# Spreading the second feed-forward blocks of a hybrid layer over its chunk steps, pass by pass

## What is computed

```python
x = x + rwkv(layernorm(x))      # projections, a recurrence along time, projection
x = x + ffn(layernorm(x))       # "F1": 512 -> 1376 gate and up, silu(gate)*up, 1376 -> 512
x = x + mamba(layernorm(x))     # projections, conv of 4 taps, state scan with 16 states, gate, projection
x = x + ffn(layernorm(x))       # "F2": the same weights as F1
```

## Time and profile before

| | |
|---|---|
| median of 3 runs | 3535.84 us (3535.15 to 3536.14) |
| the profiled execution, its own time | 3535.06 us |
| its span, first to last instruction | 3533.3 us |
| granted TensorE clock, mean | 0.969 |

### The profile page before, as it was taken

The page is one execution under the profiler, slowest core; times in us unless marked ns, Lnnn a source line. Parts: engine busy times, 40 slices in busy tenths (PEclk is TensorE's granted clock), DMA queues, the critical chain, the costliest instruction groups (busy, mean ns, idle before and its releaser), DMA issues.

```text
span 3533.3 us, 46726 instructions
## 1 busy us (share of the span) xinstructions
PE 3233.1 (92%) x12672; PEld 2341.7 (66%) x12672; DVE 3141.1 (89%) x5676; ACT 2602.2 (74%) x5260; POOL 2473.7 (70%) x1959
## 2 busy tenths in 40 slices
PE   4889899899999999999999999999999999976738
PEld 4666676676767676767767676767676767754425
DVE  5899995499999999999999999999999999999990
ACT  4777774487878787878787878788787878766650
POOL 0343444296969696969696969696969696968680
PEclk9999999999999999999999999999999999988879
DMA  3122213111111111111111112121112010111110
GB/s 107 60 75 85 77 63 129 54 34 39 42 39 41 40 40 40 42 37 42 39 41 40 42 37 48 33 49 31 52 27 58 24 55 25 54 25 36 26 35 6
DMA packets 119380, 165.39 MB, mean 47 GB/s; under 512 B 8544, under 2 KB 84192, under 8 KB 118624
## 3 DMA queue, kind: packets, MB, share of 16 engines
q1 hardware_dynamic: 119136, 162.63, 16.5%
HBM read 128.39 MB, written 25.69 MB: 44 GB/s over the span
## 4 chain that ended last, share of the span: by engine, by line
POOL 46%; issue 21%; DVE 21%; PE 6%; ACT 4%; DMA 1%; DVEq 1%; POOLq 0%; SPq 0%; ACTq 0%
POOL dBu L907 24%; POOL yacc L920 17%; DVE D L1412 6%; DVE U L1361 4%; PE W L1162 3%; DVE prod L1431 1%; DVE dBu L1392 1%; PE W L1196 1%; DVE U L1404 1%; DVE D L1434 1%; DVE sgm L1345 1%; DVE delta L1399 1%; POOL NV L305 1%; POOL EO L293 1%; POOL MX L278 1%
## 5 line engine op out<-in xcount | busy, mean ns | idle before, releaser
L907 POOL TENSOR_TENSOR dBu<-U,BC 128x512 f32<-128x512 f32 x1024 | 1297.8, 1279 | 359.9 <-DMA BC<-bc_scratch 247.3
L1412 DVE TENSOR_TENSOR_SCAN D<-D,hc,dBu 128x256 f32<-128x256 f32 x2048 | 1433.5, 738 | 17.5 <-ACT D L1077 17.5
L1162 PE MATMUL W<-nT,wffn 128*128 128x256 f32 x5632 | 1230.9, 381 | 7.8 <-ACT nT L948 7.8
L1162 PEld LDWEIGHTS W<-nT,wffn 128*128 128x128 f32 x5632 | 1063.9, 189 | 181.2 <-issue 18.3
L1077 ACT ACTIVATE D<-delta,A 128x256 f32<-128x256 f32 x2048 | 890.7, 468 | 363.4 <-DVE yacc L1444 338.7
L920 POOL TENSOR_TENSOR yacc<-yacc,prod 128x512 f32<-128x512 f32 x752 | 956.9, 1273 | 175.1 <-DVE prod L1431 171.0
L1196 PE MATMUL W<-wffn,hT 128*128 128x512 f32 (+1 forms) x1408 | 617.6, 595 | 7.9 <-DVE hT L1330 7.9
L1431 DVE TENSOR_TENSOR prod<-D,BC 128x512 f32<-128x512 f32 x752 | 503.8, 670 | 0.0
L1196 PEld LDWEIGHTS W<-wffn,hT 128*128 128x128 f32 (+1 forms) x1408 | 263.1, 190 | 326.2 <-issue 307.6
L1162 PE MATMUL W<-nT,win 128*128 128x256 f32 x2048 | 451.0, 381 | 30.1 <-ACT xext L996 22.8
L1162 PEld LDWEIGHTS W<-nT,win 128*128 128x128 f32 x2048 | 391.3, 191 | 91.1 <-ACT xext L996 23.6
(11 more groups left out here) (128 smaller groups left out, 3036.7 us busy)
## 6 DMA issues: line engine op xcount, KB each, us to landing
BC<-bc_scratch SPq DMA_DIRECT2D x256, 256.0 KB, 4.6
XM<-x_scratch SPq DMA_DIRECT2D x29, 512.0 KB, 6.0
X<-x_scratch SPq DMA_DIRECT2D x17, 512.0 KB, 3.6
ix<-idx SPq DMA_DIRECT2D x33, 255.0 KB, 2.9
X<-x SPq DMA_DIRECT2D x16, 512.0 KB, 3.4
XR<-x SPq DMA_DIRECT2D x16, 512.0 KB, 3.4
x_scratch<-XR SPq DMA_DIRECT2D x16, 512.0 KB, 3.6
out<-X SPq DMA_DIRECT2D x16, 512.0 KB, 2.8
```

The costliest lines, as they stand in the source:

```text
L907: nc.gpsimd.tensor_tensor(dBu[e % 4][:], U[:, 2 * j:2 * j + 2, :], BC[slot][:, 0:1, :].to_broadcast([P, 2, CH]), ALU.mult).then_inc(s_dBu, 1)
L1162: last = T_.matmul(dst, lhsT, rhs, start=(n == 0), stop=(n == len(terms) - 1))
L1412: V.tensor_tensor_scan(D[:, m, :], D[:, m, :], dBu[e % 4][:, m % 2, :], hc[:, n, m:m + 1], ALU.mult, ALU.add).then_inc(s_scan, 1)
```

## The change

The late F2 blocks of steps 2 to 13 are cut between passes. Over six steps five blocks are done: the late part has 6, 4, 3, 2, 1 and 0 passes, and the **rest** of the block (the missing passes and its `down`) stands first in the next step, ahead of the early block. So steps 2 to 13 hold 11/6 blocks on average in place of 2, F2 of chunks 11 to 14 are left over, and steps 14 and 15 hold two blocks each in place of one. The transposed rows of a cut block are kept in a new buffer `nT2`; `dtl`, `bcS` and `dump` share memory to make room, which adds waits on earlier uses. The rows x3 between Mamba and F2 now go through DRAM (`x3_d`): stored behind BC slot 4, loaded again into `X3` for the rest's residual (behind slot 5) and for the late norm. The early rows in `XM` give way to the next Mamba rows, whose norm is now made in the middle of the step (in place, in `XM`), and are loaded a second time for their residual (`early_slot`). The silu, norm and residual places come out of a formula in units of a place.

```diff
-F1_SILU = (10, 13, 16, 19, 22, 24)
-F1_RES = 31
-F2_SILU = (36, 39, 42, 45, 48, 50)
-F2_RES = 56
-L_SUM = 12
-M_SUM = 50
+PASS, HALF, DOWN = 3.15, 1.6, 8.8
+LEAD, LEAD_REST = 6.85, 6.5
...
+        LEAN = NC - 2
+        PART = (NP, 4, 3, 2, 1, 0)
...
         def early(i):
-            return ("F1", 1) if isinstance(i, int) and i == 0 else ("F1", i + 2)
+
+            if i == 0:
+                return "F1", 1
+            return ("F1", i + 2) if i < LEAN else ("F2", 2 * i - NC - 1)
...
+            if i == 1 or i >= LEAN:
+                return ("F2", 0 if i == 1 else 2 * i - NC), NP, True
+            turn_, n = divmod(i - 2, len(PART))
+            return (("F2", (len(PART) - 1) * turn_ + n + 1), PART[n], False) if PART[n] else (None, 0, False)
...
+        def slot(e):
+
+            return -(-e // 4) + 2
...
+                for p in range(first, last):
+                    t += HALF if p == NP - 1 else PASS
+                    out.append(t)
+                return out, t
+
+            t = LEAD
+            at["e_norm"], at["e_evac"] = 0, 6
+            if R_:
+                e, last = ends(LEAD_REST, r, NP)
+                at["r_silu"] = tuple(round(x) for x in e)
+                t = last + DOWN
+                at["r_res"] = round(t - 2.5)
...
+            e, last = ends(t, 0, NP)
+            at["e_silu"] = tuple(round(x) for x in e)
+            at["e_res"] = round(last + DOWN - 2.5)
+            at["xm_slot"] = max(3, slot(at["e_norm"] - 3))
+            at["m_sum"] = 4 * (at["xm_slot"] - 2) + 6
+            at["m_norm"] = at["m_sum"] + 6
+            at["m_evac"] = round(last) + 4
+            at["l_sum"] = max(at["m_norm"] + 2, 18, (at["r_res"] or 0) + 11)
...
+            at["early_slot"] = slot(round(last))
...
+                        if n == 4:
+                            keep_x3(i)
+                        if n == 5:
+                            if R_:
+                                load_x3(i, R_[1])
+                            elif L_:
+                                load_x3(i, L_[1])
+                        if R_ and n == at["r_slot"]:
+                            keep_out(R_, X3)
+                            if L_:
+                                sp.wait_ge(out_stored, 16 * (outs.index(R_) + 1))
+                                load_x3(i, L_[1])
+                        if n == at["early_slot"]:
...
+                            load_early(i)
...
+                    if R_:
+
+                        project(i - 1, 1, 1 - a)
+                        for p in range(n_rest, NP):
...
+                            gate_up(R_, p, nT2)
...
+                        down(R_, [(1, 4, turn_early)])
```

More of the change, by code:

```diff
@@ new lines, in hybrid_block_kernel @@
+        norms, downs = [("F1", 0), ("M", 0)], [("F1", 0)]
+        passes = [(("F1", 0), p) for p in range(NP)]
+        xm_loads, x3_loads = [("x1", 0), ("x1", 2)], [("x1", 1), ("x2", 0)]
+        for i in range(NC):
+            (R_, r_), E_, (L_, l_, whole) = rest(i), early(i), late(i)
+            if R_:
+                passes += [(R_, p) for p in range(r_, NP)]
+                downs.append(R_)
+                x3_loads.append(("rest", R_[1]))
+            norms.append(E_)
+            passes += [(E_, p) for p in range(NP)]
+            downs.append(E_)
+            if i == 0:
+                norms += [L_, ("M", 1)]
+            else:
+                norms += [("M", i + 1)] * (i + 1 < NC) + [L_] * (L_ is not None)
+            passes += [(L_, p) for p in range(l_)]
+            if whole:
+                downs.append(L_)
+            if i:
+                x3_loads += ([("late", L_[1])] if L_ else []) + [("x2", i)]
+                xm_loads += [("x2", i + 1)] * (i + 1 < NC) + [("early", i)]
+            if i + 1 < NC:
+                xm_loads.append(("next", i + 1))
@@ new lines, in hybrid_block_kernel, with gate_side @@
+        LAST_ = ("F2", NC - 1)
+        norms.append(LAST_)
+        passes += [(LAST_, p) for p in range(NP)]
+        downs.append(LAST_)
+        outs = [block for block in downs if block[0] == "F2"]
+        norm_no, down_no = norms.index, downs.index
+        pass_no = lambda block, p: passes.index((block, p))
+        xm_no = lambda what, n: xm_loads.index((what, n))
+        x3_no = lambda what, n: x3_loads.index((what, n))
+        def gate_side(i):
+            (_, r), (_, n, whole) = rest(i), late(i)
+            if whole:
+                return 0
+            if rest(i)[0]:
+                return (NP - r + n) % 2
+            return 1 - n % 2
@@ L833, in step @@
                 def step(i, back, f1, more):
+                    at = places(i)
+                    (R_, _), (L_, _, whole) = rest(i), late(i)
                     if not back:
+                        sp.wait_ge(n_done, TT * (norm_no(("M", 0)) + 1))
                         load_x1(2)
-                    elif more and not f1:
-                        sp.wait_ge(n_done, TT * (norm_no("M", i) + 1))
-                        load_x2(i + 1, NC)
                     sp.wait_ge(m_bcS, i + 1)
@@ L891, in step @@
                 def step(i, back, f1, more):
-                    at = places(f1)
-                    if f1 and not back:
-                        root(norm_no(*early(i)))
+                    at = places(i)
+                    if not back:
+                        root(norm_no(early(i)))
                     def outer(e):
@@ L1053, in step @@
                         soft(j)
[L1054 to L1058, removed]
+                    at = places(i)
+                    E_, (L_, n_late, whole), (R_, n_rest) = early(i), late(i), rest(i)
+                    early_rows, late_rows, mamba_rows = (XM, X3, XM) if back else (X3, XM, X3)
                     def save(e):
@@ new lines, in step @@
+                        if more and e == at["m_norm"]:
+                            if not back:
+                                act.wait_ge(f_h, pass_no(L_, NP - 1) + 1)
+                            slope(norm_no(("M", i + 1)))
+                            norm(norm_no(("M", i + 1)), mamba_rows, XM if back else nrm)
+                        if more and e == at["next_sum"]:
+                            act.wait_ge(xm_loaded, 16 * (xm_no("next", i + 1) + 1))
+                            sums(i, norm_no(early(i + 1)), XM)
@@ L1111, in step @@
+                        if more and e == at["next_sum"] + 1:
+                            squares(norm_no(early(i + 1)), XM)
                         if e == G_LATE:
@@ new lines, in gate_up, with down @@
+                def gate_up(block, p, src):
+                    Wp = W[sides[block, p]]
+                    for half, wt in ((0, wg), (2, wu)):
+                        for m, r in rows(p):
+                            last = chain(Wp[0:r, half + m % 2, :], [(wt[:, k, m * P:m * P + r], src[:, k, :]) for k in range(KH)])
+                    last.then_inc(f_gu, 1)
+                def down(block, turns=()):
+                    done = pass_no(block, NP - 1)
+                    o = W[down_sides[block]][:].rearrange("p (t a) n -> p t (a n)", t=TT)
+                    pe.wait_ge(f_h, done)
+                    for t in range(TT):
+                        for k in range(MI):
+                            for at_t, at_k, what in turns:
+                                if (t, k) == (at_t, at_k):
+                                    pe.wait_ge(f_h, done + 1)
+                                    what()
+                            if t == 0 and k == MI - 1:
+                                pe.wait_ge(f_h, done + 1)
+                            r = LAST if k == MI - 1 else P
+                            last = T_.matmul(o[:, t, :], hT[0:r, k, t * P:(t + 1) * P], wd[0:r, k, :], start=(k == 0), stop=(k == MI - 1))
@@ new lines, in step @@
+                    for p in range(n_late):
+                        if p == 0:
+                            pe.wait_ge(n_T, norm_no(L_) + 1)
+                        elif p == 1:
+                            pe.wait_ge(f_res, down_no(E_) + 1)
+                        else:
+                            pe.wait_ge(f_h, pass_no(L_, p) - 1)
+                        gate_up(L_, p, nT2 if back else nT)
+                    if whole:
+                        down(L_, [] if back else [(1, 6, lambda: turn(norm_no(("M", 1)), f))])
@@ L1369, in step @@
                 def step(i, back, f1, more):
-                    at = places(f1)
+                    at = places(i)
+                    E_, (L_, n_late, whole), (R_, n_rest) = early(i), late(i), rest(i)
+                    early_rows, late_rows = (XM, X3) if back else (X3, XM)
                     for h in range(2):
```

537 lines of the change are left out of this document (313 added, 224 removed).

## The result

The changed kernel takes 3620.94 us (median of 4, 3614.63 to 3621.76) against 3535.52 us: the ratio is 1.0238, 95% interval 1.022 to 1.0255. It is slower, as I had thought likeliest, but by 85 us where I had 12; the range ended at 3562.

A forecast was written before the change was run, and what follows sets the result against it. PE was taken to set the pace, with DVE 5 us behind; small gains and losses per step and -1 for a head summed to +11.7 us, giving a median of 3547.5 us (+0.33%), range 3515 to 3562.

The forecast's parts named there:

- The sum of 11.7 us: Whole kernel: the step changes and a shorter head behind step 14 add up to +11.7 us, median 3547.5.
- my own case: Whole kernel: the main forecast of 3547.5 us, +0.33%, own range 3541 to 3556, chance 0.40.
- PE sets the pace: Step 5's loop: PE busy 144.95 of 145.50 us sets the pace, with DVE only 5 us behind.
- The first bound: Loops of steps 2 to 13: each gains at most its waits, 5.3 us, and what DVE no longer does.
- The waits forecast where squares stand ahead of a silu: Steps 5, 6, 11, 12: squares share a silu's place, ahead of it; the same meeting before cost DVE 2.67 us.
- Where the places put the waits: Steps 1 to 15: DVE waits on PE at residuals; PE's saving shows only after a step's last such meeting.
- this meeting: Steps 1, 2, 8: DVE meets the early down's end at residual place 30, at 72.7 us, hiding M's norm work.
- Steps 14 and 15: Last two loops: one more block gives DVE busy 144.6 and 144.4, waits taken as 4.9: +3.8 and +4.4 us.
- Steps 4 to 7 and 10 to 13: Loops with less PE work: -2.1 in 4 and 10, +0.7 in 5 and 11, +0.6 in 6 and 12, -1.5 in 7 and 13.
- The first (faster, 3515): Rows land in 3.6 us, ACT works off extras in its lead; 3515, or 3500 if residual meetings cost nothing; chance 0.28.
- The second (work only changes its step): DVE, not PE, sets the pace: 8.8 us leave and 8.8 come, so no change, 3536; chance 0.22.
- The third (SP held): SP's queue: a store's or norm's wait delays a BC slot, POOL and DVE wait, 2.8 us in ten steps: 3575; chance 0.10.

The follow-up runs named there:

- Experiment 11: The kernel before, blocks not cut, with early residual, late means, squares and norm, and Mamba means moved to other places: 3512.41 us.
- Experiment 10: The changed kernel with ACT's norm work on one column (not the layer's output) and the fifth silu one place earlier: 3558.63 us.
- experiment 9: The changed kernel with 16 unneeded matmul instructions on TensorE ahead of the early block's last pass, in steps 1 to 15: 3601.05 us.

## Why the prediction was wrong

**Right, or nearly.** The sum of 11.7 us adds up; the upper end of my own case does not (the bounds given make 3558, not 3556). "PE sets the pace" was nearly right: I read it from 144.95 of 145.50 us busy, though DVE never waited for TensorE in that loop. Experiment 11 shows that TensorE's bound is 143.9; the last 1.6 us were DVE's waits for ACT, which TensorE filled with work for the next step. DVE's work does not change (3141.1 us in both). The first bound, that a loop can gain its waits and DVE's saved work, held: the best loop is 140.3 of 145.5. The waits forecast where squares stand ahead of a silu are in the trace at their places, 1.9 us at place 32 of step 5 and 2.8 at 35 of step 6 (I had the 2.67 of the kernel before). So is the wait for x3 at place 13 (5.9; I had 6.2), the waits at the rest's residual (1.9 to 3.3; I had 2.5 in step 4), and DVE's new wait for `XM` behind a DMA in step 5 (1.9; I had 2.5). That the kernel got slower is thus no luck, but these waits are the smaller part of it: 46 of the 86 us lie in steps 1, 2, 8, 14 and 15, where I had 9.

**The step that failed** is the one under "Where the places put the waits": I took TensorE's timeline as free-running up to each residual (72.7 in step 1, 101.5 in step 4) and let DVE's waits on the way be hidden by it ("they cost no more than this meeting hides"). But `down` starts only with the fifth product, which is DVE's and is behind ACT's. In step 1 the products' waits held TensorE for 5.24 us, the lower clock cost 2.8 more, and the meeting came at 80.2. Experiment 10, which takes away ACT's norm work inside the passes and moves the fifth product forward, gives the 72.5 of my sum; experiment 9 shows the clock's part by itself.

**Five terms that were mis-sized or missing.** (1) I gave the fifth silus' shift from 22 to 23 and from 48 to 49 no price at all, though both rows of places stand in the table; it cost 26 us over the kernel. (2) The clock: I had used it only to take 1 us off behind step 14 (that head fell by 0.5); over the fifteen early `down`s it took TensorE 29 us more than at the full clock, and experiment 9, which avoids nearly all of that, was 20 us faster. (3) Steps 14 and 15: I took the waits of a step like 5; they were those of step 1 on top of DVE's larger work, +13.3 and +10.6 for +3.8 and +4.4. (4) Steps 4 to 7 and 10 to 13, where TensorE's saving was to show after the last meeting, met the same chain: TensorE waited 2.6 to 3.6 us ahead of their early `down`, and the loops were 0.3 to 6.0 us longer. (5) The collision that I priced in steps 5 and 6, squares ahead of a silu in one place, also stands at place 19 of steps 1, 2, 8, 14 and 15; I had not seen it there, and it cost DVE 2.28 us at place 18.

**The rivals.** The first (faster, 3515) had the right limit but not for this kernel: its case without waits at the residuals gave 3500, and with the places mended the kernel comes to 3493. The second (work only changes its step) is wrong: at equal care for the places, the cut blocks are 18 us ahead. The rule of the Trainium skill named there ("Perfetto Trace Analysis", Identifying the Most-Contended Engine) judges TensorE by the weight loads' busy share (and by the share of its peak rate, which no row here gives): 104.01 of 143.90 us or 72% in experiment 11, against 98% for DVE. By it DVE and not TensorE is the engine to relieve. The runs agree only in part: relieving TensorE was worth 1.5 us a loop, up to where DVE was the bound. The third (SP held) did not come: POOL waited for BC only in the heads, as before (20.6 us behind step 1), and in no loop.

**What stays open.** How much of the loss the added transfers carry through ACT's waits was not tested in the changed kernel itself. What decides whether the clock falls after a wait of a given length is not shown. And how much of the 18 us for cutting would be left if both kernels' places were searched further was not tried.

## What to carry to other kernels

When two engines hand work back and forth, one's waits are not cover for the other's: before calling a wait hidden, follow what the waiting engine owes to the engine that hides it, and when. In an order written by hand, price each operation's place like an instruction: here one place of a silu (26 us) and two of a residual (42 us) each outweighed the whole saving in matmuls (18 us). A change of structure should be judged with its places mended, and against the old structure with the same mending.

## What the runs showed of the hardware

With a wait of 5.24 us ahead of `down`, in a TensorE that had been full before it, the granted clock fell to 0.50 (918.8 to 925.6), and the 14 matmuls behind the wait took 9.05 us for 6.28. With 16 unneeded matmul instructions ahead, and 1.82 us of wait left, the clock stayed at 1.00 and the kernel was 20 us faster (one run): extra work on the fullest engine paid. The length of the wait does not settle it: after 3.57 us the clock stayed in step 5 and fell in step 11 of the same execution.
